# Order of loads, of PSUM reads and of sign sums in a seven-product matrix kernel (AdaLN feed-forward with grouped convolution)

## What is computed

```python
# x (32, 64, 1024), cond (32, 128), bias (64,), weight (64, 16, 9), c_weight (64, 128), kernel (1024, 1024) bool, scale ()
conv = conv1d(x, weight, padding 4, 4 groups)            # (32, 64, 1024)
conv = conv + (cond @ c_weight.T)[:, :, None] + bias[None, :, None]
out  = x + scale * einsum('bsi,if->bsf', conv, kernel * 2.0 - 1.0)
```

## Time and profile before

| | |
|---|---|
| runs | 168.71, 169.67, 169.59 us; median 169.59 |
| profiled execution | 169.47 us, its span 167.6 us (1.9 us lie around the span) |
| granted TensorE clock | 0.998 |
| busy, share of the span | TensorE 160.4 us (96%), VectorE 137.8 (82%), ScalarE 72.4 (43%), GpSimd 45.8 (27%) |

### The profile page before, as it was taken

One profiled execution on the slowest core, in us unless ns is written; L12 is line 12 of the kernel. 1 busy time (PEld: TensorE's weight loads), 2 busy tenths in 40 slices (PEclk: granted clock), 3 DMA queues, 4 the chain that ended last, 5 costly groups with the idle time before them and its releaser, 6 DMA issues.

```text
span 167.6 us, 2766 instructions
## 1 busy us (share of the span) xinstructions
PE 160.4 (96%) x910; PEld 135.1 (81%) x910; DVE 137.8 (82%) x180; ACT 72.4 (43%) x66; POOL 45.8 (27%) x51
## 2 busy tenths in 40 slices
PE   7999999999799979999999999999999999999993
PEld 2579888998796859987898889887998879888782
DVE  4736694879999999779996899679976999779944
ACT  3327696171882047520790169223772071204200
POOL 5622864008220604006310344015400713000000
PEclk9999999999999999999999999999999999999999
DMA  5889989688879889698878988897988682806014
GB/s 200 252 177 280 381 187 174 108 206 203 163 215 256 223 178 380 148 242 214 229 252 211 268 154 324 208 246 143 301 211 247 99 285 53 198 0 246 8 73 177
DMA packets 27421, 34.03 MB, mean 203 GB/s; under 512 B 3632, under 2 KB 19440, under 8 KB 27408
## 3 DMA queue, kind: packets, MB, share of 16 engines
q1 hardware_dynamic: 21600, 25.36, 55.0%
q10 hardware_dynamic: 5232, 7.30, 16.4%
q0 software_dynamic: 576, 1.20, 3.2%
HBM read 10.19 MB, written 8.40 MB: 111 GB/s over the span
## 4 chain that ended last, share of the span: by engine, by line
PE 38%; DVE 22%; DMA 13%; ACTq 11%; issue 7%; ACT 3%; SPq 3%; DVEq 0%
ACTq L502 11%; DMA y_sum<-y_two 11%; DVE sums L659 9%; PE ps_A L883 8%; PE ps_conv L837 7%; DVE lo L669 5%; PE ps_conv L864 5%; PE ps_C L883 4%; DVE x_nat L680 4%; PE ps_A L793 4%; SPq L255 3%; DMA x_nat<-x 3%; ACT x_phase L476 3%; PE ps_C L899 2%; PE ps_A L899 2%
## 5 line engine op out<-in xcount | busy, mean ns | idle before, releaser
L437 POOL TENSOR_TENSOR set<-x_blk 128x512 f32<-128x512 f32 x14 | 19.9, 1438 | 61.3 <-DMA x_blk<-x_phase 61.3
L521 ACT CAST hi<-sums 128x1024 fp32r<-128x1024 f32 x14 | 14.7, 1049 | 42.3 <-DVE sums L659 36.4
L680 DVE SCALAR_TENSOR_TENSOR x_nat<-ps_A,scale_col,x_nat 128x512 f32<-128x512 f32 x27 | 20.2, 747 | 12.9 <-PE ps_A L883 12.2
L476 ACT COPY x_phase<-x_nat 128x1032 f32<-128x1032 f32 x13 | 27.2, 2135 | 3.8 <-issue 3.8
L883 PE MATMUL ps_A<-sign_T,hi 128*128 128x512 f32 x80 | 22.1, 397 | 0.3 <-issue 0.3
L521 ACT CAST hi<-y_sum 128x1024 fp32r<-128x1024 f32 (+1 forms) x14 | 11.7, 833 | 23.9 <-DMA y_sum<-y_two 16.3
L883 PE MATMUL ps_A<-sign_T,lo 128*128 128x512 f32 x80 | 21.5, 391 | 0.0
L864 PEld LDWEIGHTS ps_conv<-toeplitz,set 128*128 128x128 f32 x168 | 19.8, 192 | 0.6
L864 PE MATMUL ps_conv<-toeplitz,set 128*128 128x128 f32 x168 | 19.9, 275 | 0.0
L437 POOL TENSOR_TENSOR w_bytes<-x_blk 128x512 f32<-128x512 f32 x12 | 12.3, 1050 | 22.5 <-DVE sums L659 18.6
L864 PE MATMUL ps_conv<-toeplitz,w_bytes 128*128 128x128 f32 x144 | 17.1, 276 | 1.0 <-ACT w_bytes L488 1.0
(11 more groups left out here) (109 smaller groups left out, 238.5 us busy)
## 6 DMA issues: line engine op xcount, KB each, us to landing
x_nat<-x SPq DMA_DIRECT2D x16, 512.0 KB, 4.4
out<-x_nat SPq DMA_DIRECT2D x15, 512.0 KB, 4.9
x_blk<-x_phase SPq DMA_DIRECT2D x114, 64.5 KB, 3.1
y_sum<-y_two ACTq DMA_DIRECT2D x52, 128.0 KB, 3.2
w_bytes<-w_bool SPq DMA_DIRECT2D x2, 512.0 KB, 6.0
x_blk<-x_phase POOLq DMA_DIRECT2D x8, 64.5 KB, 3.6
shift<-shift_dram POOLq DMA_DIRECT2D x2, 256.0 KB, 5.4
x_blk<-x_phase ACTq DMA_DIRECT2D x6, 64.5 KB, 4.4
```

Source lines behind the costliest of these rows:

```text
L437: nc.gpsimd.tensor_tensor(dif[r][:, e], x_blk[r][:, :, e:e + M:2], x_blk[r][:, :, e + 1:e + 1 + M:2][:, :, 0:K], ALU.subtract).then_inc(di ...
L476: nc.scalar.copy(x_phase[r][:, :, 0:M + 1], line(d, r, 0, PAD + L + PAD).rearrange("r (m q) -> r q m", q=B)).then_inc(phase_ok[r], B)
L521: nc.scalar.copy(parts(hi_all, k), group(k)).then_inc(hi_ok[k], 1)
L680: nc.vector.scalar_tensor_tensor(there, bank[b], scale2_col[:, :], there, ALU.mult, ALU.add).then_inc(summed[k], 1)
```

## The change

Five edits:

1. TensorE's last two plain products of double 0 change places: A21 B12 (bank E) runs before A21 B11 (bank C). VectorE reads E where it read C, and C in step 1 behind C11_P1, where E had been read later in the step.
2. SP: for d = 0 the load of the first pair of double 3 is issued behind the blocks of the second pair of double 2, not ahead of them.
3. VectorE: C21_A (the read of P4) goes from the head of the next step to a place between C12_C and S2. C11_P1 comes before C11_P2, which moves behind the first fast_y (in step 1 behind C22_A). S4 comes ahead of low_part(S12).
4. VectorE: the first half of T4 is made between the two add_shift calls of pair 3, in double 0, and not in step 1.
5. GpSimd's pacing wait for r = 1 is on the low part of S1 and S2 in place of S4.

```diff
-         ("A11", "B12", "B"), ("A21", "B11", "C"), ("A21", "B12", "E"))
+         ("A11", "B12", "B"), ("A21", "B12", "E"), ("A21", "B11", "C"))
-PLAIN_DONE = {"A": 5, "B": 6, "C": 7, "E": 8}
+PLAIN_DONE = {"A": 5, "B": 6, "E": 7, "C": 8}
@@ SP
                     to_blocks(d + 2, 0)
-                    load(d + 3, 0, x_in[0]) if runs(d, 6) else None
+                    if runs(d, 6) and d > 0:
+                        load(d + 3, 0, x_in[0])
                     to_blocks(d + 2, 1)
-                    load(d + 3, 1, x_in[1]) if runs(d, 6) else None
+                    if runs(d, 6):
+                        if d == 0:
+                            load(3, 0, x_in[0])
+                        load(d + 3, 1, x_in[1])
@@ GpSimd
-                    pool.wait_ge(s_ok["S4"], d - 1)
+                    pool.wait_ge(lo_ok["S12"], d - 1)
@@ VectorE, sum_up
-                before = {"C11_P1": "C11_P2", "C22_A": "C22_C", "C12_C": "C12_A"}.get(k)
+                before = {"C11_P2": "C11_P1", "C22_A": "C22_C", "C12_C": "C12_A"}.get(k)
@@ VectorE, first_double
-                plain_sum("C")
+                plain_sum("E")
                 add_shift(1, 1, 0)
+                last_signs(slice(0, KH // 2))
                 add_shift(1, 1, 1)
@@ VectorE, last_signs
-                dve.wait_ge(plain_done, len(PLAIN))
+                dve.wait_ge(plain_done, 7)
@@ VectorE, step
                 if d > 1:
-                    sum_up("C21_A", d - 1)
                     combine("S3", d)
+                    combine("S4", d)
                     low_part("S12", d)
-                    combine("S4", d)
-                if d > 1:
-                    sum_up("C11_P2", d)
                     sum_up("C11_P1", d)
                 if runs(d, 2):
                     fast_y(d + 1, 0)
                 if d == 1:
+                    sum_up("C11_P1", d)
+                    plain_sum("C")
+                else:
                     sum_up("C11_P2", d)
-                    sum_up("C11_P1", d)
                 low_part("A22", d)
                 if runs(d, 2):
                     fast_y(d + 1, 1)
-                if d == 1:
-                    plain_sum("E")
-                    last_signs(slice(0, KH // 2))
...
                     sum_up("C22_A", d)
+                    if d == 1:
+                        sum_up("C11_P2", d)
                     low_part("A", d + 1)
                     combine("S1", d + 1)
                     sum_up("C12_C", d)
+                    sum_up("C21_A", d)
                     combine("S2", d + 1)
```

More of the change, by code:

```diff
@@ L703, in plain_sum, with last_signs @@
                                                ).then_inc(plain_summed[b], 1)
+            def last_signs(u):
+                dve.wait_ge(sign_ok["B21"], KH)
+                dve.wait_ge(plain_done, 7)
+                sign_sums("T4", plain("B21", u), ALU.subtract, plain("T2", u), u)
             def first_double():
@@ L739, in first_double @@
                 low_part("S12", 1)
-            def last_signs(u):
-                dve.wait_ge(sign_ok["B21"], KH)
-                dve.wait_ge(plain_done, len(PLAIN))
-                sign_sums("T4", plain("B21", u), ALU.subtract, plain("T2", u), u)
             def step(d):
                 if d > 1:
-                    sum_up("C21_A", d - 1)
                     combine("S3", d)
+                    combine("S4", d)
                     low_part("S12", d)
-                    combine("S4", d)
-                if d > 1:
-                    sum_up("C11_P2", d)
                     sum_up("C11_P1", d)
```

## The result

The changed kernel is slower: median 172.1 us of six runs against 169.5, ratio 1.0149 (95% interval 1.0103 to 1.0195). I had forecast 169.3 and gave slower by over 1% a chance of 0.14. Its profiled execution took 171.27 us (before 169.47), its span 169.4 (167.6).

What follows compares the result with a forecast made beforehand. TensorE, busy 96%, was taken as the bound, with only its gaps to win. The terms -1.83 (step 1), +0.97 (four steps) and +0.61 (last step) summed to -0.25: 169.2 us, 169.3 against the median, range 167.2 to 171.3.

Steps and rivals of the forecast that it cites:

- What bounds the kernel: TensorE, busy 96% of the span, so only its gaps, opening and tail can be won; P1 waits 1.8 us for VectorE.
- part 1's chain: Doubles 2 to 6: P4, C21_A, S2, high_part(S12), odd_blocks, next convolution; the wait moves from P1 to the convolution, 6.03 behind P4.
- rival 1: The odd copy doesn't hold the convolution (d+1, 0), so the stalls just go: 165.8 us; chance 0.12.
- Part 2: Double 0 and step 1: first mark (start of the convolution ending step 1) at 61.6 against 63.43, -1.83 us.
- the 0.55 between 61.05 and 61.6: Step 1: convolution start with S1 and S2 undisturbed by GpSimd, 61.05, against the 61.6 taken.
- rival 4: SP's change wins nothing and the moved load makes the phases (3, 0) late: step 1's mark near 63.0, 170.7 us; chance 0.06.
- The 0.5 for SP's edit: Double 0: blocks (2, 1) issued earlier on SP, so the convolution (2, 1) starts 0.5 earlier, at 45.22; bounds 0 and 0.62.
- Part 1's size: Four middle steps of 18.66 each, 74.64 against 73.67: +0.97 us, bounds -0.23 and +0.97.
- rival 3: GpSimd comes ahead of the low part of A, 0.78 more per such step; 171.6 for three, 172.4 for four; chance 0.15.
- Part 3: Last step: C21_A waits for P4 and S2's 0.61 comes behind it, delaying P3: +0.61 us, bounds 0.4 and 0.7.
- Part 4: The remaining edits cost nothing: GpSimd's pacing wait, C11_P1 ahead of C11_P2 (P1 readable at 5.62, VectorE there at 5.9).

Runs made afterwards that it cites:

- experiment 1: Changed kernel with ScalarE's odd_blocks queued ahead of high_part(S12): 0.9972 of the kernel before, where the changed kernel stands at 1.0149.
- f2: Changed kernel with SP's order of before (load (3, 0) ahead of the blocks (2, 1)), run beside the changed kernel: 1.0097 of the kernel before.
- f0: The changed kernel itself, run again on another chip: 1.0116 of the kernel before.
- a2: Changed kernel with SP's order of before, the first of two such runs: 1.0083 of the kernel before.
- c1: Kernel before with one edit, C21_A between C12_C and S2 in every step: 1.021 of the kernel before.
- c3: Kernel before with C21_A ahead of S2 and ScalarE's odd_blocks ahead of high_part(S12): 1.0149 of the kernel before.
- c5: Kernel before with C21_A ahead of S2 and C11_P1 ahead of C11_P2, which moves behind the first fast_y: 1.0237 of the kernel before.
- f3: Changed kernel with C21_A behind S2 again and SP's order of before: 0.9962 of the kernel before.
- experiment 7: Changed kernel, odd_blocks moved, SP's old order, S2 ahead of C21_A in last step: 0.9864, 0.9847; also C11_P2 ahead of C11_P1 there: 0.9842; SP's new order: no ratio.
- b1: Kernel before with SP's edit alone: 0.9931 of the kernel before.
- a3b: Changed kernel with C21_A behind S2 again, second run of this version: no ratio, the one time left is 168.85 us.
- a3: Changed kernel with C21_A behind S2 again in every step: no ratio, the one time left is 168.41 us.
- d1: Changed kernel with C21_A behind S2 again and odd_blocks ahead of high_part(S12): 1.0117 of the kernel before.
- d2: Changed kernel with odd_blocks ahead of high_part(S12) and S2 ahead of C21_A in the last step, SP's new order kept: no ratio, one time left, 166.51 us.
- a1: Changed kernel with ScalarE's odd_blocks queued ahead of high_part(S12): 0.9972 of the kernel before.
- a6: Changed kernel with odd_blocks ahead of high_part(S12), SP's order of before, and S2 ahead of C21_A in the last step: 0.9864 of the kernel before.

## Why the prediction was wrong

- **What bounds the kernel** and **part 1's chain** were right: P1's waits went and the convolution's came, at 5.99 behind P4 where 6.03 was forecast. Moving the odd copy (experiment 1) shows the chain, and rival 1, that the copy has enough slack, is out. The three misses, 1.02, 0.96 and 0.11, all lie on one side and make the 2.09 between -0.25 and +1.84.
- **Part 2 is the step that failed**, by 1.02. S1 was put at 56.05 with no term for its data, the y transfers, and the late load was let shift the blocks (3, 0) and GpSimd by at most 0.7. The convolution (2, 1) (44.93) and P4 (54.98) came even earlier than forecast, but S1 waited for a y transfer and started at 57.13, 1.08 late, which is the whole miss: that GpSimd lay on S2 (1.22 long, not 0.68) was allowed for in the 0.55 between 61.05 and 61.6. The issue of the load moved from 35.82 to behind 41.43, the phases (3, 0) began 1.18 later, the y transfers 1.51 later and GpSimd 1.57 later (57.43). ScalarE's phases wait for the load, the eight issues of y stand behind them and the high part behind those; this was taken as parallel. It is nearest to rival 4 (mark near 63.0, chance 0.06). How much of the 1.02 is the load's stays open: f2 without the late load has its mark 1.09 earlier than f0, but a2, also without it, has it later than the changed kernel.
- **The 0.5 for SP's edit** in part 2 isn't shown either. Up to the convolution (2, 1) c1, c3 and c5 run the code of the kernel before, and it starts at 45.13, 45.96 and 44.79 (before 45.72); f2 and f3, with SP's old order, have it at 45.0. The scatter between executions is larger than the term, so its coming at 44.93 was in part luck.
- A smaller miss of part 2: in double 0 GpSimd started 0.55 earlier (37.23 against 37.78) and came ahead of the low part of A (37.40, 1.95 long), and P2 waited 0.33.
- **Part 1's size** was too small, by 0.96. A step took 18.73, not 18.66: from the mark to P4 it was 12.74 in place of 12.63, a refill of TensorE behind the wait of the convolution that I had put at nothing. And in the fourth step GpSimd (130.36) came ahead of the low part of A (130.58, 1.90 long): 19.42. That is rival 3, which I had priced at 0.78 for each such step and measured at 0.69. In the second trace of the changed kernel (f0) no step had it, and the four took 74.59 against the forecast 74.64. So it comes and goes between executions.
- **Part 3** had the size (P3 9.81 behind P4, forecast 9.8), the other 0.1 being the same refill, and half the cause. C21_A waited 0.48 for P4 as forecast (the row below the list), but S2 in its old place gave nothing back. C11_P1 ahead of C11_P2 costs the same 0.6 there, as VectorE then stands before a P1 that isn't done (experiment 7). Part 4 had called that edit free, "VectorE gets there at 5.9", which is true of the middle steps and not of the last. That the size came out is luck in part.
- **SP's edit alone** gained 0.7%, within the changed kernel nothing that can be measured: gains measured on one order of this loop, where VectorE meets GpSimd by tenths of a microsecond, didn't add up in another.
- **The range.** Its top, 171.3, is 2.0 above the forecast, so the profiled execution (171.27) only just stayed inside, and the median of the runs lies 0.8 above that execution. Why it does isn't shown. The forecast's own range, 168.3 to 170.4, isn't what the bounds of its parts add up to: with GpSimd ahead of S1 these give some 168.5 to 170.0.

```profile
152.96 0.75 DVE L684 SCALAR_TENSOR_TENSOR x_nat<-ps_A,scale_col,x_nat 128x512 f32<-128x512 f32 x1 [0.48 <-PE ps_A L887]
```

## What to carry to other kernels

When a read is moved ahead to free a bank, follow every in-order queue that waits for what it was moved past: here a copy for another unit, two places behind on ScalarE, paid for it, and moving that copy ahead of the cast that waits was worth more (1.8%, or 1.4% by the second measurement) than the change was to bring. An instruction whose data are long ready (C21_A, S3, C11_P2) may be there to fill the time of another engine's cast or of a product still running; before it is moved, look what the queue would wait for without it, and treat the last iteration by itself. A transfer put back in a queue can be late for its whole chain of readers, and that chain has to be walked up to the instruction that was to gain. And look at single executions beside the ratio: SP's edit gained 0.7% alone, and went with a lowered clock and some 3% more time in a third of them.

## What the runs showed of the hardware

A VectorE sum of two SBUF operands took 0.68 or 1.53 depending on whether GpSimd had begun a subtraction just before it: S1 took 1.53 when it started 0.16 behind GpSimd (76.24 and 76.08, kernel before) and 0.69 when it started 0.27 ahead (75.02 and 75.29, b1). The Trainium skill (SBUF — State Buffer, Who interferes with whom) has this as exclusion by order of issue, and these rows agree. Not expected was that holding GpSimd back moves the cost on, to S4 and the low part, and gains nothing (1.0159).

After a long idle time TensorE's granted clock fell. In the profiled execution of a3b (173.04 us) P1 waited 2.75 us, and the stretches from 78 to 90 us read (columns: stretch, its length, busy time of PE, PEld, DVE, ACT, POOL with counts, PEclk, DMA share, GB/s):

```profile
78.00:81.00 3.00, 0.44 (x2) 0.42 (x3) 3.00 (x6) 1.17 (x2) 0.00 (x0) 1.00 1.01 170
81.00:84.00 3.00, 3.00 (x11) 2.44 (x10) 2.09 (x4) 3.00 (x5) 1.08 (x2) 0.56 0.96 354
84.00:87.00 3.00, 3.00 (x26) 3.00 (x25) 1.84 (x4) 3.00 (x2) 0.98 (x1) 0.87 0.33 119
87.00:90.00 3.00, 3.00 (x27) 2.91 (x26) 2.96 (x5) 0.47 (x1) 0.00 (x0) 1.00 0.81 147
```

The clock is near its lower level (1.2 of 2.4 GHz) right behind the gap and back at full behind 87. Gaps of 2.50 (a3), 2.83 (d1) and 2.45 us (d2) were each followed by a stretch of 2 us at 0.50, the lower level itself; gaps of 1.39 us (a1) and 1.53 us (a6) left it at 1.00.
